# Six PSUM banks for the steps' sums, and a later load of the last expert's first weights, in a graph and expert kernel

## What is computed

```
aggr = segment_sum(edge_weight[:, None] * layernorm(x)[dst], src, 3125)
x    = x + gnn_mlp_and_norm(aggr + (1 + eps) * layernorm(x))
xn   = layernorm(x)
top2, w = top-2 of softmax(xn @ Wr + br), renormalised
x    = x + sum over the two experts e of w[e] * (gelu(ln_e(xn) @ W1[e] + b1[e]) @ W2[e] + b2[e])
```

## Time and profile before

| | us |
|---|---|
| median of 3 runs | 1275.2 |
| lowest and highest run | 1272.94, 1278.61 |
| profiled execution | 1274.54 |
| its span | 1272.8 |

### The profile page before, as it was taken

How to read it: one execution, slowest core, us unless ns; L and a number is a source line. 1 busy time by engine, 2 the same in 40 slices (tenths; PEclk the granted TensorE clock), 3 DMA queues, 4 the chain that set the end, 5 groups by cost and what they waited for, 6 DMA issues and landing times.

```text
span 1272.8 us, 26947 instructions
## 1 busy us (share of the span) xinstructions
PE 893.7 (70%) x6929; PEld 613.4 (48%) x6930; DVE 735.5 (58%) x1653; ACT 679.8 (53%) x2186; POOL 661.5 (52%) x673
## 2 busy tenths in 40 slices
PE   2383288566666465654777765884369999999995
PEld 1131143234333232332566544774357787777883
DVE  4674178565866455564555565896835555555553
ACT  7884199327685267852333412663335555555552
POOL 3835666464665666656666419120525454454442
PEclk9995599767897678887656778895589999999998
DMA  4114222234222332323444312363012322322322
GB/s 123 62 48 135 87 82 78 61 92 100 85 87 75 92 87 84 90 77 91 134 145 151 111 54 93 102 190 111 1 59 42 49 44 47 49 43 48 50 42 25
DMA packets 59620, 102.56 MB, mean 81 GB/s; under 512 B 10298, under 2 KB 43048, under 8 KB 59400
## 3 DMA queue, kind: packets, MB, share of 16 engines
q0 software_dynamic: 29520, 65.96, 21.1%
q1 hardware_dynamic: 30008, 35.55, 8.7%
HBM read 84.27 MB, written 17.20 MB: 80 GB/s over the span
## 4 chain that ended last, share of the span: by engine, by line
PE 45%; DVE 17%; ACT 10%; issue 8%; another core or an unknown queue 8%; DVEq 2%; DMA 1%; POOL 0%; POOLq 0%; ACTq 0%
PE bank L1055 7%; ACT Wall L1141 6%; PE bank L1041 4%; PE bank L1043 4%; PE bank L1042 4%; PE bank L896 4%; PE bank L894 3%; PE bank L1057 3%; ACT RB L1149 3%; DVE RA L1633 3%; PE bank L907 3%; PE bank L895 3%; PE bank L858 2%; DVE Wall L1633 2%
## 5 line engine op out<-in xcount | busy, mean ns | idle before, releaser
L726 POOL DMA_INDIRECT Wall<-xl_d,gbuf x391 | 388.5, 994 | 272.1 <-SPq L595 147.2
L1149 ACT ACTIVATE RB<-RB,gbuf 128x128 f16<-128x128 f16 x488 | 178.8, 424 | 283.9 <-DVE RB L1620 259.6
L894 PE MATMUL bank<-Wall,RB 128*128 x488 | 165.7, 339 | 139.9 <-DVE Wall L1633 54.1
L1141 ACT ACTIVATE Wall<-Wall 128x128 f32<-128x128 f16 (+1 forms) x782 | 247.1, 383 | 26.7 <-DVE Wall L1548 25.2
L1633 DVE TENSOR_TENSOR RA<-RA,bank 128x256 f32 x244 | 101.8, 417 | 253.0 <-remote 127.8
L1271 ACT ACTIVATE RA<-bank,b1T 128x128 f32<-128x128 f32 x448 | 127.7, 368 | 121.1 <-PE bank L1043 119.6
L786 POOL DMA_INDIRECT out_dram<-RA,slot_tok x56 | 99.7, 1780 | 162.3 <-ACT RA L1277 138.0
L858 PE MATMUL bank<-Wall 128*128 128x512 f16 (+1 forms) x391 | 153.7, 440 | 39.1 <-ACT Wall L1141 26.0
L1041 PE MATMUL bank<-RA,Wall 128*128 128x128 f16 x896 | 175.4, 221 | 0.4 <-issue 0.2
L1043 PE MATMUL bank<-RA,Wall 128*128 128x128 f16 x896 | 175.3, 221 | 0.0
L1042 PE MATMUL bank<-RA,Wall 128*128 128x128 f16 x896 | 175.2, 221 | 0.0
(11 more groups left out here) (319 smaller groups left out, 1585.2 us busy)
## 6 DMA issues: line engine op xcount, KB each, us to landing
stage<-in_L_ffn_W SPq DMA_DIRECT2D x10, 1024.0 KB
Wall<-xl_d,gbuf POOLq DMA_INDIRECT x391
Wall<-in_L_ffn_W SPq DMA_DIRECT2D x6, 1024.0 KB, 6.5
Wall<-in_x SPq DMA_DIRECT2D x4, 640.0 KB, 7.4
xl_d<-Wall SPq DMA_DIRECT2D x4, 640.0 KB
out_dram<-RB SPq DMA_DIRECT2D x4, 640.0 KB
xn_d<-RA SPq DMA_DIRECT2D x4, 640.0 KB
RB<-in_x SPq DMA_DIRECT2D x1, 1792.0 KB
```

The lines of the kernel that those rows point to most:

```text
L726: pool.indirect_dma_start(out=ring[:, t % RING * 2 * D:(t % RING + 1) * 2 * D], out_offset=None, in_=xl_d, in_offset=bass.IndirectOffsetOn ...
L894: mm(o, high, ring[:, bass.ds(at, D)], start=True, stop=False)
L1141: last = act.activation(hi_word[:, n % SR, k * S:(k + 1) * S], hi_hot[:, n // HB % 2, n % HB // 2, 0:S, n % 2], ACT.Copy, scale=pay[k][:, ...
L1149: act.activation(low, high, ACT.Copy, scale=rec_r[:, n:n + 1]).then_inc(sw_built, 1)
```

## The change

From step 232 on, pair p takes bank 1 + (p - 116) mod 6, that is banks 1 to 6. `added_before` says how many sums must have been added before PE may write to a pair's bank again. Step 232 gains two waits, for the last reader of banks 4 and 5 (`place_taken`) and of bank 6 (`steps_ready`). Apart from that, the load of expert 7's first weights stands behind the last release in SP's order; before, it stood ten releases earlier, ahead of the release of tile 349.

```diff
+        def agg_bank(pair):
+
+            wide = pair - SB[2] // 2
+            return 1 + pair % 3 if wide < 0 else 1 + wide % 6
+
         def agg_out(n):
 
-            return bank[1 + n // 2 % 3][:, n % 2 * D:(n % 2 + 1) * D]
+            return bank[agg_bank(n // 2)][:, n % 2 * D:(n % 2 + 1) * D]
+
+        def added_before(pair):
+
+            users = [q for q in range(pair) if agg_bank(q) == agg_bank(pair)]
+            return 2 * users[-1] + 2 if users else 0
...
-            return (T0[1] + 12, T0[-1] - 8)[e] if e < 2 else T0[-1] + 10 * e - 9
+            return (T0[1] + 12, T0[-1] - 8)[e] if e < 2 else T0[-1] + 10 * e - 9 if e < NE - 1 else EC
...
-                if n % 2 == 0 and n >= 6:
-                    pe.wait_ge(agg_added, n - 4)
+                if n == SB[2]:
+                    pe.wait_ge(place_taken, sum(groups(j) for j in range(NCH)))
+                    pe.wait_ge(steps_ready, NCH)
+                if n % 2 == 0 and added_before(n // 2):
+                    pe.wait_ge(agg_added, added_before(n // 2))
```

## The result

The changed kernel takes 1269.7 us (median of 12 runs, 1266.2 to 1271.3) against 1274.1 us of the kernel before (12 runs in the same sitting, 1272.4 to 1278.6). The ratio is 0.9963, with an interval of 0.9951 to 0.9974. So the gain is 4.4 us, real but under half of the 11 us forecast. The profiled executions differ by about as much: spans of 1267.9 and 1272.8 us.

The account below looks back on a forecast made before the run. It took holds as the bound: PE's completion reports reach DVE late while gathers are issued. From 1275.2 us, -9 (first stretch), -2 (last chunk) and 0 (load) gave 1264 us; range 1246 to 1280, the forecast's own 1258 to 1268.

Parts of the forecast that it names:

- the sum's first and largest term: First stretch from step 232: six banks let PE lead further, cutting a third of POOL's 27.0 us of pauses; -9 us.
- the -2 us of the last chunk: Last chunk: six banks save an eighth of POOL's 16.6 us of pauses; -2 us, bounds 0 and -8.
- Rival 1: Steps from 232: SP's releases set POOL's runs, so its pauses stay; 1275 us, chance 0.30 together with the change not taking.
- the change that does not take: PE waits mostly for words or matrices of ACT, so its lead does not grow; 1275 us, chance 0.30 with rival 1.
- The load: Expert 7's weights, issued behind ten more releases: -5.7 + 4.1 + 1.5 = 0 us, bounds -5.7 and +11.
- The hold: Step 450: PE's completion report, held while the last ten gathers are issued, delays the addition; 5.7 us that go.
- The quiet stretch: 715 to 726 us, few gathers, additions 0.92 us each; with gathers at 1.26 us, 12 additions cost 4.1 us more.
- The two new waits: Step 232: they wait for counts complete a chunk earlier, so they cost 0 us.
- The sign of error: Prediction is wrong if anything before 449 us or after the last addition differs by more than 2 us.
- Rival 2: Expert 7's load comes late because holds delay SP's releases; +11 us, 1286 us without gain from the banks; chance 0.12.
- Rival 3: Ten steps of lead nearly end the holds and POOL becomes the bound; -37 us, 1238 us; gains beyond forecast up to it 0.13.
- The rule of the Trainium skill: PE's completion counts: about 26 ns each, so four steps of lead reach DVE within 0.2 us; sum about 0, 1275 us.

Follow-up runs that it names:

- the pairs: Changed kernel with SP releasing two tiles at once: last two chunks 1266.5 us beside the changed kernel's 1268.9; all four chunks 1254.8 us against 1265.1 of the kernel before.

## Why the prediction was wrong, and its sign right

The forecast was 11 us less, all of it from the banks. The banks alone gave nothing, and the load alone, which had been priced at 0, gave 2.3 and 3.7 us of the 4 or so. That the kernel got faster at all, and that 1269.7 us lies in the wide range of 1246 to 1280, is luck and not a merit of the sum.

**The step that failed** is the sum's first and largest term, "I take a third off the 27.0 us: -9 us", and with it the -2 us of the last chunk. Its reasons were that DVE would find more finished sums behind each wait, and that "a longer burst of releases gives POOL a longer run". PE did get ahead. The timeline of the changed kernel shows what became of it:

```profile
593.32 0.95 POOL L736 DMA_INDIRECT Wall<-xl_d,gbuf  x1 [0.30 <-issue]
...
594.38 0.27 PE L909 MATMUL bank<-Wall,RB 128*128 x1
...
596.45 0.27 PE L909 MATMUL bank<-Wall,RB 128*128 x1 [1.13 <-issue]
...
598.00 0.42 DVE L1646 TENSOR_TENSOR RA<-RA,bank 128x256 f32 x1 [4.20 <-PE bank L909]
...
599.17 0.39 PE L907 MATMUL bank<-Wall,RB 128*128 x1 [2.44 <-issue]
...
602.36 0.42 PE L909 MATMUL bank<-Wall,RB 128*128 x1
603.74 0.42 DVE L1646 TENSOR_TENSOR RA<-RA,bank 128x256 f32 x1 [4.84 <-PE bank L909]
```

DVE's addition of 598.00 is step 348's. Its pair was finished at 586.30, and PE stands before step 360. DVE had older sums to add until 593.8 and then stood idle for 4.20 us. The count that let it go on came 11.7 us after the matmul; for the next pair, finished at 587.56 and added at 603.74, it was 16.2 us. Twelve finished steps lie there, and more of them makes no difference. And PE, which now has banks to work on with, has gaps in a hold that no count ends ("issue"), here of 1.1 and 2.4 us. I had read PE's 5.70 us at a full bank as time in which it would have worked at its unheld pace. In the first stretch POOL's waits for SP went from 39.7 to 40.2 us. The term measured 0: banks alone 1264.95 us against 1264.98, with an interval that allows 1.5 us of gain or 2.4 us of loss.

The rule behind it, that a hold lasts until POOL runs dry, holds mostly but not always: at 598.00 POOL is in the middle of a run, with gathers at 597.08 and 598.33. From 449 to 763 us of this execution DVE waited 18 times for over 2 us on a pair that had been finished over 2 us before; 16 of these waits ended 1.1 to 2.1 us after the end of POOL's last gather, two while it gathered on. Which of the two is the cause stays open, since POOL stops for want of the same count.

**Rival 1** had the outcome of this part: the pauses stay and the banks give nothing. Its reason, that SP's releases set how POOL runs, is a small part of the truth, as the pairs show: with half the work SP stands waiting for the count, and POOL gains some 3 us of 165. I gave it, with the change that does not take, 0.30 and took as the evidence against it "PE's 21.2 us of waits for DVE". Those waits were real, and 14 us less of them changed no time. That is the lesson of this case.

**The load** was priced at 0, from -5.7 + 4.1 + 1.5. In the two profiles of the result it measured as follows. The hold: -5.5 us (15.65 to 10.17 from issue to addition), as forecast. The quiet stretch lost: +3.4 us (from step 440's addition to the load, 718.8 to 722.95 before and 717.0 to 724.49 now) for 4.1. The load's lateness behind its bias: 0 for 1.5. The six steps after the resumption took 1.9 us less, a term that the sum did not have: the next product took 1.84 us in place of 3.54, at a granted clock of 1.00 (the level of 2.4 GHz) in place of 0.50 (1.2 GHz). The steps from 456 on took 1.3 us more. That is -2.8 us; the remaining -1.8 us stand before step 440 already, half of them before step 232, where nothing was changed. One pair of executions carries such terms only roughly. In the side-by-side runs the load alone gave -2.3 and -3.7 us, the whole change -4.1. That is within its bounds, -5.7 and +11. The sum priced two things too dear, the quiet stretch and the lateness, and left one out.

**The two new waits** cost nothing to be seen, nor does the stricter wait for sums at step 232, which the prediction passed over: PE stood 4.61 us for it, but DVE's addition of step 232 comes 2.9 us after that of step 231, as before, at 455.9 us for 456.8. The sign of error set at 2 us before 449 us did come: single additions before step 232 lie up to 4.6 us earlier and 4.1 us later than in the kernel before. Since the change touches nothing there, this is how much two executions with holds can differ in place, and the sign was set too tight. After the last addition the two agree: 509.6 us from there to the end before, 509.3 now. The additions end at 758.2 us, where the prediction had 752.

**Rival 2**, the late load, did not come in any run with the moved load; in each of them with a profile the load was issued within 0.5 us after the end of its bias (at most 717.79 to 718.24). Its case leaned on a hold "as long as 12.70 us at its worst", but of these 12.70 us of DVE's wait only 5.74 us lie after the end of PE's matmul; before that PE itself waited for the weights and made the product. **Rival 3** needed DVE to run dry seldom; it ran dry 27 times for the 18 at most that my forecast wanted.

**The rule of the Trainium skill** that I weighed (*TensorE: Matmul & The Clock Gate*, "The cost: per-tile semaphore tail", about 26 ns an increment) gave a sum of about 0. As a picture of how counts arrive it agrees with the traces where no gathers hold them: 0.13 us from matmul to sum in the kernel without gathers. Where they are held, its premise fails. That the sum worked out from it, about 0, was the right one for the banks is luck as well, since the reason is another.

## What to carry to other kernels

A large wait of a producer for buffers (21 us here) is worth nothing if the consumer stands before finished sums; ask what ends the consumer's wait, and whether two engines resume on the same count at once. Where counts were late, deeper buffers did not help. Less work on the queue that hands buffers back helped a little here (half the releases in two chunks: 2.4 us beside the changed kernel). And measure the same kernel in more than one sitting before tuning to a stall: these holds, 113 us of 1265, were absent in two sittings of seven.

## What the hardware showed beyond that

- The same program on the same inputs took 1152 us in two sittings and 1265 to 1274 us in five. The difference, 113 us in six banks alone, is all between the first and the last addition, where GpSimd issues its gathers.
- While gathers are issued with holds, increments of SP's queue that take 17 ns otherwise take up to 728 ns in the stretches shown; without gathers, or in a sitting without holds, all of them take 17 ns there. With half the releases none took over 323 ns, and the holds stayed.
- In the changed kernel DVE, idle, got the count of a finished pair 11.7 us after the end of its matmul, and of the next pair 16.2 us after.
- Waiting, ahead of every fourth gather, for the one before it to land cost 2.3 us for each such wait (52 of them, 120 us).
